# Two feature blocks turned by moves, five flags instead of three, and two woven steps in a one-core adaLN block

## The reference

```python
mod = (_silu(L0_c) @ L0_wmod).reshape(L0_c.shape[0], 6, 1, -1)
sa, ca, ga, sb, cb, gb = (mod[:, i] for i in range(6))
ga = (2 * (ga >= 0) - 1) * jnp.maximum(jnp.abs(ga), 0.25)     # gb likewise
h = _layernorm(x) * (1 + ca) + sa
x = x + ga * (h @ (weight * block_mask).T)                     # weight 512 x 512
h = _layernorm(x) * (1 + cb) + sb
gate = (h @ Wg.T) * ag                                         # Wg, Wu: 1376 x 512
up = (h @ Wu.T) * au
out = ((_silu(gate) * up) @ Wd.T) * ad                         # Wd: 512 x 1376
x = x + gb * out
```

## Time and profile before

| | |
|---|---|
| median of 3 runs | 175.0 us (174.76 to 175.45) |
| the profiled execution | 175.16 us, of which the traced span is 173.4 us |
| TensorE busy | 166.5 us, 96% of the span, granted clock 0.997 on average |
| VectorE, ScalarE, GpSimd busy | 111.7, 80.9, 27.8 us |
| DMA | 24.00 MB, mean 138 GB/s |

### The profile page before, as it was taken

How to read it: one execution, slowest core, us unless ns; L and a number is a source line. 1 busy time by engine, 2 the same in 40 slices (tenths; PEclk the granted TensorE clock), 3 DMA queues, 4 the chain that set the end, 5 groups by cost and what they waited for, 6 DMA issues and landing times.

```text
span 173.4 us, 2502 instructions
## 1 busy us (share of the span) xinstructions
PE 166.5 (96%) x860; PEld 126.7 (73%) x860; DVE 111.7 (64%) x234; ACT 80.9 (47%) x113; POOL 27.8 (16%) x32
## 2 busy tenths in 40 slices
PE   6799989999999999999999999999999999999992
PEld 6755444465468888887888888888888888888781
DVE  6968956995756999878865595437544313442574
ACT  3034005458799956875356533454324534252200
POOL 1324402950069110000000000008300000000000
PEclk9999999999999999999999999999999999999998
DMA  5999977999999302440000002001400000000015
GB/s 170 365 408 404 401 219 190 397 409 353 413 406 388 109 4 51 104 94 0 6 0 4 0 4 89 33 4 69 179 0 4 0 4 4 2 0 4 4 62 182
DMA packets 12774, 24.00 MB, mean 138 GB/s; under 512 B 3056, under 2 KB 5360, under 8 KB 12368
## 3 DMA queue, kind: packets, MB, share of 16 engines
q1 hardware_dynamic: 11040, 22.03, 35.2%
q10 hardware_dynamic: 1712, 1.66, 3.2%
HBM read 19.74 MB, written 2.11 MB: 126 GB/s over the span
## 4 chain that ended last, share of the span: by engine, by line
PE 90%; DMA 4%; SPq 2%; DVE 2%; issue 1%
PE bank L1009 46%; PE bank L1079 20%; PE bank L980 17%; DMA modw<-in_mod_ln 4%; PE bank L888 3%; PE bank L1065 2%; PE bank L959 2%; SPq L287 1%; SPq L293 1%; DVE xt L878 0%; DVE xn L789 0%; DVE xt L869 0%; DVE xn L875 0%; PE bank L943 0%; PE bank L933 0%
## 5 line engine op out<-in xcount | busy, mean ns | idle before, releaser
L1009 PE MATMUL bank<-ht,whi_gu 128*128 128x512 f32 x352 | 83.5, 391 | 0.0
L1009 PEld LDWEIGHTS bank<-ht,whi_gu 128*128 128x128 f32 x352 | 65.6, 188 | 13.8 <-issue 0.5
L770 DVE SCALAR_TENSOR_TENSOR awork<-bank,scal,awork 128x512 f32<-128x512 f32 x22 | 16.5, 749 | 44.0 <-PE bank L1009 40.4
L1079 PE MATMUL bank<-whi_dn,in_split 128*128 128x512 f32 x148 | 37.2, 391 | 0.1
L528 ACT ACTIVATE awork<-bank,scal 128x512 f32<-128x512 f32 x22 | 15.2, 690 | 45.6 <-PE bank L1009 45.6
L1079 PEld LDWEIGHTS bank<-whi_dn,in_split 128*128 128x128 f32 x148 | 27.6, 188 | 6.2 <-issue 0.4
L980 PE MATMUL bank<-awork,wffn 128*128 128x512 f32 x64 | 30.6, 604 | 0.2 <-DMA modw<-in_mod_ln 0.2
L473 ACT ACTIVATE whi_gu<-wffn 128x1024 fp32r<-128x1024 f32 x22 | 23.3, 1058 | 6.6 <-PE bank L1009 6.6
L980 PEld LDWEIGHTS bank<-awork,wffn 128*128 128x128 f32 x64 | 11.0, 190 | 10.9 <-issue 9.5
L779 DVE TENSOR_TENSOR in_split<-awork,in_split 128x512 fp32r<-128x512 f32 x21 | 16.5, 785 | 0.7
L466 ACT ACTIVATE junk<-wffn 128x1536 uint8<-128x1536 uint16 x11 | 16.2, 1476 | 1.1 <-DMA wffn<-in_w_down 1.0
(11 more groups left out here) (85 smaller groups left out, 118.3 us busy)
## 6 DMA issues: line engine op xcount, KB each, us to landing
wffn<-in_w_gu SPq DMA_DIRECT2D x10, 512.0 KB, 8.6
modw<-in_mod_ln SPq DMA_DIRECT2D x6, 512.0 KB, 7.0
wffn<-in_w_down SPq DMA_DIRECT2D x10, 256.0 KB, 10.2
xt<-in_x SPq DMA_DIRECT2D x8, 256.0 KB, 5.8
modw<-in_mod_gate SPq DMA_DIRECT2D x2, 1024.0 KB, 13.8
maskt<-in_att_mask SPq DMA_DIRECT2D x4, 256.0 KB, 7.9
awork<-in_att_w SPq DMA_DIRECT2D x4, 256.0 KB, 8.1
modw<-in_mod_ln SPq DMA_DIRECT2D x1, 1024.0 KB, 6.9
```

Of the source, the lines that this page charges most:

```text
L770: dve.scalar_tensor_tensor(inner[:, s % 2, :], bank[gu_bank(s, 1)][:, :], scal[:, c, 1:2], silu_g[:, s % 2, :], ALU.mult, ALU.mult).then_i ...
L1009: return pe.matmul(bank[gu_bank(s, u)][:, :], w, h, start=(k == 0 and part == 0), stop=(k == KT - 1 and part == 1))
L1079: last = pe.matmul(bank[4 + t][:, :], h, w, start=(c == 0 and part == 0), stop=(c == C - 1 and part == 1))
```

## The change

The flags become five, for the chunks 0 to 2, 3, 4 and 5, 6 and 7, and 8 to 10. Each is the maximum over all chunks up to its group's end. GpSimd takes the maximum over the partitions and compares (`make_flag`); the small matmuls on TensorE and VectorE's reading of them go. The feature blocks 2 and 3 of q = 2 are turned by moves: `normalise(2)` writes features 0 to 255 into `xn` as before and features 256 to 511 in blocks of 32 into the gates' place, SP issues eight moves and ScalarE four, VectorE copies the diagonal (`keep_second`) and turns the blocks (`transpose_second`). The chunks from 3 on are loaded behind SP's moves. Steps 0 and 1 are one run of 32 products, ordered by feature block, in `gate_up_first`. GpSimd clears the tail of the last chunk after its additions for sample 1 instead of before. The mask's fourth product moves behind `columns(2)` and to bank 6.

```diff
-BLK_BANK = [7, 6, 7, 7]
+BLK_BANK = [7, 6, 7, 6]
+BY_SYNC_SECOND = 8
+BY_PE = 2
-CHECKS_AT = {0: 1, 1: 1, 2: 1, 3: 1, 4: 1, 5: 1}
-FLAG_VECTOR_AT = {1: 1, 6: 2}
-GROUPS = [(0, 3), (3, C - HELD), (C - HELD, C)]
+CHECKS_AT = {0: 1, 1: 1, 2: 1, 3: 1, 4: 1, 5: 2, 6: 1}
+FLAG_VECTOR_AT = {3: 2, 5: 3, 7: 4}
+GROUPS = [(0, 3), (3, 4), (4, 6), (6, 8), (8, C)]
...
+        xq1 = gates[:, NB:2 * NB, :].rearrange("p b n -> p (b n)").rearrange("p (j n) -> p j n", j=GRP)
+        xb1 = xn[:, :, BY_PE * P:D]
+        xturn_second = modw[:, 2, 0:KT - BY_PE, :]
...
+        def move_second(eng, n):
+            i, j = MOVES[n]
+            eng.dma_start(xb1[BLK * j:BLK * (j + 1), i, :], xq1[BLK * i:BLK * (i + 1), j, :])\
+               .then_inc(d_second[j], 16)
...
             for c in range(C):
+                if c == GROUPS[0][1]:
+                    sp.wait_ge(xn_ok, XN_FIRST + 2 * TT)
+                    for n in range(BY_SYNC_SECOND):
+                        move_second(sp, n)
                 if c == TURN_CHUNK:
                     sp.wait_ge(h_ok, 2 * TT)
                 if c == H1_CHUNK:
+                    sp.wait_ge(h_ok, 3 * KT)
...
+            def make_flag(g):
+                pool.wait_ge(flagv_ok, g + 1)
+                pool.tensor_reduce(flagm[0:1, g:g + 1], flagv[:, g:g + 1], AX_C, ALU.max).then_inc(flag_max, 1)
+                pool.wait_ge(flag_max, g + 1)
+                pool.tensor_scalar(flags[0:1, g:g + 1], flagm[0:1, g:g + 1], 0.0, None, ALU.is_gt)\
+                    .then_inc(flag_ok, 1)
...
+                if b == 1:
+                    pool.wait_ge(att_done, NB * TT)
+                    pool.memset(wffn[:, C - 1, :], 0.0).then_inc(tail_zero, 1)
                 inverse_deviation(2 + b, 0)
                 inverse_deviation(2 + b, 1)
-                if b == 0:
-                    pool.wait_ge(att_done, NB * TT)
-                    pool.memset(wffn[:, C - 1, :], 0.0).then_inc(tail_zero, 1)
+                for g in ((2, 3, 4) if b else (0, 1)):
+                    make_flag(g)
...
             check_chunk(next(check_at))
+            act.wait_ge(xn_ok, XN_FIRST + 2 * TT)
+            for n in range(BY_SYNC_SECOND, len(MOVES)):
+                move_second(act, n)
             modulate(8)
             modulate(9)
             check_chunk(next(check_at))
+            round_gu(0)
+            round_gu(1)
             modulate(10)
             modulate(11)
-            round_gu(0)
-            check_chunk(next(check_at))
-            check_chunk(next(check_at))
...
-                if s + 1 < STEPS:
+                if 0 < s < STEPS - 1:
                     round_gu(s + 1)
...
+                    if q == 2:
+                        head = slice(0, BY_PE * P)
+                        dve.tensor_scalar(xn[:, t, head], src[:, head], mv[:, q, t, 0:1], rstd[:, q, t:t + 1],
+                                          ALU.subtract, ALU.mult).then_inc(xn_head, 1)
...
+            for j in range(GRP):
+                keep_second(j)
             split(8)
             split(9)
             flag_vector(0)
+            transpose_second(2)
+            transpose_second(3)
             split(10)
-            read_flag(0)
             split(11)
-            dve.tensor_copy(onecol_r[:, :], onecol[:, 0:1].to_broadcast([P, 2])).then_inc(ones_r_ok, 1)
+            flag_vector(1)
...
-                pe.wait_ge(h_ok, 11)
+                pe.wait_ge(h_ok, NB * KT + BY_PE)
                 def products(native):
-                    for k in range(KT):
+                    for k, s in ((0, 0), (0, 1), (1, 0), (1, 1), (2, 0), (3, 0), (2, 1), (3, 1)):
+                        if (k, s) == (0, 1):
+                            pe.wait_ge(wgu_hi, 2)
...
-                    if (k, t) == (2, 0):
-                        transposes(10)
-                    if (k, t) == (2, 3):
-                        transposes(11)
-                        pe.wait_ge(modc_ok, SETS)
-                        flag_sum(0)
```

More of the change, by code:

```diff
@@ L29 @@
 AX_XY = mybir.AxisListType.XY
+AX_C = mybir.AxisListType.C
 P = 128
@@ L230, in adaln_block @@
         kept_ok = sem("kept_ok")
+        d_second = [sem(f"d_second{j}") for j in range(GRP)]
+        kept_second = sem("kept_second")
         d_turn = [sem(f"d_turn{j}") for j in range(GRP)]
@@ L446, in modulate @@
                         act.wait_ge(h_lo, n - 9)
+                turned = q == 2 and k >= BY_PE
                 src = [bank[4 + n % 2][:, :], xturn[:, k, :], bank[n % 2][:, :], xn[:, k, :]][q]
+                if turned:
+                    src = xturn_second[:, k - BY_PE, :]
                 part = slice(0, SEQ)
@@ L555, in _ @@
                 dve.memset(blkones[s, s], 1.0).then_inc(consts_ok, 1)
-            dve.memset(onecol[:, :], 1.0).then_inc(consts_ok, 1)
             scale_rows = ident[:, 0:2 * KT * NB].rearrange("p (k v b) -> p v b k", v=2, b=NB)[:, 0, :, :]
@@ L606, in keep_in_place, with keep_second, transpose_second @@
                 dve.tensor_copy(xb0[own, j, :], xq0[own, j, :]).then_inc(kept_ok, 1)
+            def keep_second(j):
+                own = slice(BLK * j, BLK * (j + 1))
+                dve.wait_ge(xn_ok, XN_FIRST + 2 * TT)
+                dve.wait_ge(x1_ok, TT)
+                dve.tensor_copy(xb1[own, j, :], xq1[own, j, :]).then_inc(kept_second, 1)
+            def transpose_second(k):
+                if k == BY_PE:
+                    for j in range(GRP):
+                        dve.wait_ge(d_second[j], 16 * (GRP - 1))
+                    dve.wait_ge(kept_second, GRP)
+                    dve.wait_ge(rows_done, SETS)
+                    dve.wait_ge(xt_done, 2 * TT + BY_PE)
+                dve.transpose(xturn_second[:, k - BY_PE, :].rearrange("p (t i c) -> p i t c", t=TT, c=BLK),
+                              xb1.rearrange("p i (t k c) -> p i t k c", t=TT, c=BLK)[:, :, :, k - BY_PE, :])\
+                   .then_inc(xt_done, 1)
             def transpose_first(k):
@@ L751, in flag_vector @@
             def flag_vector(g):
-                a, z = GROUPS[g]
+                z = GROUPS[g][1]
                 dve.wait_ge(checked, z)
-                dve.tensor_reduce(flagv[:, g:g + 1], chk[:, a:z], AX_X, ALU.max)\
+                dve.tensor_reduce(flagv[:, g:g + 1], chk[:, 0:z], AX_X, ALU.max)\
                    .then_inc(flagv_ok, 1)
-            def read_flag(g):
-                dve.wait_ge(flag_done, g + 1)
-                dve.tensor_scalar(flags[0:1, g:g + 1], bank[3][0:1, 0:1], 0.0, None, ALU.is_gt)\
-                   .then_inc(flag_ok, 1)
             def ffn_inner(s):
@@ L808, in _ @@
             normalise(1)
-            sum_mask(3)
             for j in range(GRP):
                 keep_in_place(j)
+            sum_mask(3)
+            mod_columns(2)
             keep_blocks(3)
-            mod_columns(2)
             gate_sums()
@@ L936, in mask_blocks @@
                 pe.wait_ge(msum_ok, k + 1)
-                pe.wait_ge(consts_ok, 6)
-                if k == 1:
-                    pe.wait_ge(rows_copied, 2)
+                pe.wait_ge(consts_ok, 5)
+                if k % 2:
+                    pe.wait_ge(rows_copied, 2 if k == 1 else 3)
                 elif k:
@@ L950, in transposes @@
                 if k == 0:
-                    pe.wait_ge(xn_ok, XN_FIRST + TT * q if q else TT)
+                    pe.wait_ge(xn_head if q else xn_ok, TT)
                 if n == 2:
@@ L983, in linear @@
                     last.then_inc(att_done, 1)
-            def flag_sum(g):
-                pe.wait_ge(flagv_ok, g + 1)
-                if g == 0:
-                    pe.matmul(bank[3][0:1, 0:1], flagv[:, 0:1].bitcast(F32), onecol[:, 0:1],
-                              start=True, stop=True).then_inc(flag_done, 1)
-                    return
-                if g == 1:
-                    pe.wait_ge(ones_r_ok, 1)
-                    pe.wait_ge(inner_ok, 2)
-                pe.matmul(bank[3][0:1, 0:2], flagv[:, g:g + 1], onecol_r[:, :], start=True, stop=True)\
-                  .then_inc(flag_done, 1)
             general = []
@@ L1022, in products @@
                             for u in range(2):
-                                last = gate_up_product(0, u, k, part, native)
+                                last = gate_up_product(s, u, k, part, native)
                                 if k == KT - 1 and part == 1:
@@ L1037, in products @@
                     for u, done in ((0, gate_mm), (1, up_mm)):
-                        if u == 1 and s > 1:
+                        if u == 1:
                             pe.wait_ge(silu_ok, s)
@@ L1045, in products @@
                         last.then_inc(done, 1)
-                if s == 1:
-                    pe.wait_ge(h_ok, 12)
-                else:
-                    pe.wait_ge(inner_ok, s - 1)
+                pe.wait_ge(inner_ok, s - 1)
                 with pe.If(general[GROUP_OF[c]]):
@@ L1195, in _ @@
                     gate_up_first()
-                else:
+                elif s > 1:
```

(3 more changed lines are left out.)

25 lines of the change are left out of this document (12 added, 13 removed).

## The result

The changed kernel takes 176.60 us, the median of five runs (175.68 to 177.32), against 174.76 for the kernel before in the same job: 1.0101 times as long, 95% interval 1.0079 to 1.0122. Run again later, beside other kernels, it took 176.31 against 175.11, 1.0075 (1.0049 to 1.0102). It is slower by about 0.9%. Ratios leave out executions in the chip's slow state, of which there were two in the whole study: one of the kernel before (213.53 us) and one of a later kernel (177.31 us).

The account below looks back on a forecast made before the run. TensorE's unbroken run was taken as the bound. Flag 2 (+2.8 us), flag 3 (+0.6) and the third flag's product (-0.4) made +3.0, so 178.2 profiled, 178.0 as median; range 175.0 to 186 us.

Parts of the forecast that it names:

- the forecast's own range: Total time if the main forecast of 178.0 us holds: from 176.2 to 180.3 us, chance 0.48.
- What TensorE is spared: On TensorE: eight second-layer transposes and three flag products gone, 1.52 us in all, 1.00 of it ahead of step 0.
- Z: GpSimd's work per flag: maximum over partitions 1.0 us, comparison 0.2, 0.1 between; 1.3 us, bounds 0.3 and 2.1.
- Rival A: GpSimd's reduction takes 3 to 5 us, counted at several flags: +13 us, 188 us at Z = 4; chance 0.15.
- Step 0 held by flag 0: Start of step 0 on TensorE: flag 0's way takes 0.71 of the 1.00 us gained, start at 49.05 us.
- The woven start: Steps 0 and 1 on TensorE: moves hidden; VectorE's first inner product 6.14 us after step 0 starts, instead of 4.32.
- Rival D: Moves of second-layer x land after block 2 is wanted, step 0 1 to 2 us later: 179.5 us; chance 0.05.
- Flag 2: Before step 4: flag's vector stands behind VectorE's full stretch of 12.1 us, so step 4 starts 2.8 us later.
- Flags 3 and 4: Later steps on TensorE: flag 3 usable 0.6 us late, before step 6; flag 4 taken as in time.
- Rival B: TensorE's clock falls in the gap before step 4, some 2 to 4 us more: 180 to 182 us; chance 0.14.
- Rival C: Flag 2 is no wait before step 4 and TensorE keeps what it is spared: 173.6 to 174.2 us; chance 0.08.

Follow-up runs that it names:

- flag 2 early: Changed kernel with flag 2's vector one inner product earlier on VectorE, in step 2 instead of step 3: 175.47 us, 1.0049 of the kernel before.
- after: The changed kernel itself, with the whole change, against the kernel before: 176.60 us (1.0101), again 176.31 us (1.0075).
- the woven kernel with early flags: Changed kernel, steps 0 and 1 still woven, flags 2 and 3 early, step 2's weights rounded first: 175.30 us, 1.0026 of the kernel before.
- flags alone, early: Kernel before with only the five GpSimd flags, vectors of flags 2 and 3 early, no moves or weaving: 173.84 us (0.9930), again 173.81 (0.9951).
- the flags alone: Kernel before with only its three flags replaced by five through GpSimd, no moves or weaving: 174.75 us, 0.9999 of the kernel before.
- the reduction twice: Changed kernel with GpSimd's maximum over the partitions made twice for each flag: 181.25 us, 1.0353 of the kernel before.

## Why the prediction came true, step by step

Forecast 178.0 us, measured 176.60, inside the range, and slower, with flag 2 as the cause. The mechanism held; its size was 1.8 us too large (+3.0 forecast, +1.19 from the second rows): 1.2 at step 4 and 0.6 at flag 3. The range was wide, and 176.60 lies near the lower end of the forecast's own range from 176.2. The medians of the first job differ by 1.84 us, where the profiles give 1.19 from the second rows; those of the second job differ by 1.20, where they give 1.07. So the first pair of medians makes the forecast look better than its sum was, which is luck.

- **What TensorE is spared.** Nearly right: 0.88 for the transposes and 0.40 at the third flag, as put. The first flag's product cost 0.31 and not 0.12, since it also held up the products behind it (3.63 against 3.44), so 1.2 us are spared ahead of step 0. Of all this only the flags' share, 0.84 us, shows in a median, when flags 2 and 3 are early; the 0.88 of the transposes, though TensorE has them, do not.
- **Z, the GpSimd work for a flag.** The mis-sized term. Taken as 1.3 us; the reduction takes 0.32, the comparison 0.21, and 0.08 lies between: 0.61. I placed the reduction above the 128x2 instruction because it crosses partitions; it lies well below it, and below the 0.5 to 1.5 us named as its sign. The estimate from the figure of the Trainium skill (GPSIMD Engine Reference, section 3.2), 0.12 us for the reduction and 0.4 us for Z, was the nearer one, and 0.2 too low. Rival A is out.
- **Step 0 held by flag 0.** 0.71 us expected; 0.09 of idle time and 0.30 in the first matmuls came. This execution is 0.76 ahead of the one before by 28.00 us, and the flag's vector at 45.19 is 0.7 earlier than worked out, so on time. From it to step 0 took 2.28 us instead of 3.15 (0.15, 0.1, Z, 0.1 and 1.5), and 0.7 of the difference is Z.
- **The woven start.** Step 0 to the inner product was 6.39 us (6.14 expected). The moves landed 2.5 us sooner than expected, of which 0.8 is the earlier start and 0.8 the landing of the last, 1.3 us after its issue instead of 2.1. That they were hidden was right, and the weaving was not needed for it: without it the 48 matmuls run through as well. Rival D is out.
- **Flag 2.** VectorE's stretch to the vector took 12.41 us (12.1). From vector to step 4 it took 2.00 and 0.29 more in the matmuls, against 3.15: 0.7 of the difference is Z, the rest the load and branch (1.15 us from the written flag to the matmul, with the 0.29 1.44, where 1.5 and 0.1 were put). Step 4 begins 1.3 us late from the second rows, and with the 0.29 in its matmuls is 1.6 late, instead of 2.8. TensorE is idle 1.6 us, not "2 to 4". That the wait at step 2 vanishes in it was shown.
- **Flags 3 and 4.** Flag 3 was expected 0.6 late and is in time, again by Z; there is no idle stretch before step 6. Flag 4 was taken as in time and is, but only because of the gap before step 4: with flag 2 early it costs 1.0 us, the most of the three. The prediction counted the instructions ahead of its vector and left out that the first of them waits for moves, 3.15 us there.
- **Rival B.** Given 0.14. It did not happen in the changed kernel (gap 1.6 instead of 3 us) and did where the gap reached 2.95, at 1.3 us, and once at 1.87, at 1.6 us, both less than the 2 to 4 put on it.
- **Rival C.** Not seen with flag 2 where it is. Its times, 173.6 to 174.2 us, are reached with other edits: early flags, and steps 0 and 1 apart or no moves.

What stays open: the median of after in its first job is 0.9 us above its fastest, profiled execution. Between its two profiled executions such a difference is all in the landing of the inputs, and the same holds for the profiled execution of the woven kernel with early flags; for the executions without a profile it is not shown. That the first inner product and the additions meet differently from one execution to the next (its cast and subtraction took 0.82 and 1.66 us in one, 0.63 and 1.67 in the other) is only 0.2 us.

The best kernel of the study is the smallest edit: five flags through GpSimd, with flag 2's vector one inner product earlier and flag 3's ahead of the second gate's products of step 4 instead of behind them, at 0.9930 and 0.9951 of the kernel before.

## What to carry to other kernels

When a branch or a flag has to reach a busy engine, follow the flag back to the queue position of its first instruction: here three lines that put two instructions of 0.15 us earlier on VectorE were worth about as much as all the products spared. An engine that is full sets the time of everything put behind it, and so does one that idles for a transfer, as VectorE does ahead of flag 4. A gap closed at one flag shows up at the next, so each later one has to be followed again.

## What the runs showed of the hardware

- A maximum over 128 partitions of one column takes GpSimd 0.31 us and the comparison of one number 0.20; beside VectorE's cast and subtraction (flags alone, early: at 62.89 and 63.46 us) they took 0.49 and 0.68.
- From a flag's writing to the first matmul behind the branch on an idle TensorE: 1.15 us in after, 1.15 with the flags alone, 1.24 with the reduction twice. At full clock the 16 matmuls behind it then take 0.29 to 0.31 us more than in a run without a gap.
- VectorE's cast of 128x512, usually 0.44 us, lasted 3.07 beside GpSimd's additions and memset.
- TensorE's clock was granted at half after 2.95 us of idle time, and in one execution after 1.87, while in an execution of another kernel 1.88 left it whole.
